# Layer 2's preparation of the states taken into the sixteen steps of its experts, with a new table of search steps

## What is computed

```
x = layer0(x)              # delta-rule attention, three cycles of a coupling net as gate
x = layer1(x)              # two blocks: time mix, windowed attention, gated FFN
# layer 2
u  = silu(conv4(x_proj_half));  sg = silu(other half)
dt, B, C = rmsnorm(x_proj @ u)          # 64 + 16 + 16 rows
dt = softplus(dt_proj @ dt + b);  du = dt * u
h_n = scan(exp(dt * A_n) * h_n + du * B_n),  y = sum_n h_n * C_n     # 16 states n
experts = sum_e w2_e(silu(w1_e x) * (w3_e (gate_e x)))               # 4 experts, 4 chunks each
x = x + silu(experts) * out_proj((y + D u) * sg)
# layer 3: 16 heads; of every score row only the 25 largest stay (found as 4 x "eight largest")
```

## Time and profile before

| what | value |
|---|---|
| median of 3 runs | 5127.44 us (5120.69 to 5140.48) |
| profiled execution, own time | 5138.43 us |
| its span | 5136.6 us |
| mean granted clock of TensorE | 0.837 of 2.4 GHz |
| busy over the span | TensorE 3962.0 us (77%), VectorE 3993.4 (78%), ScalarE 2973.6 (58%), GpSimd 2537.6 (49%) |

### The profile page before, as it was taken

One profiled execution on the slowest core, in us unless ns is written; L12 is line 12 of the kernel. 1 busy time (PEld: TensorE's weight loads), 2 busy tenths in 40 slices (PEclk: granted clock), 3 DMA queues, 4 the chain that ended last, 5 costly groups with the idle time before them and its releaser, 6 DMA issues. The chain is left out here.

```text
span 5136.6 us, 59306 instructions
## 1 busy us (share of the span) xinstructions
PE 3962.0 (77%) x17112; PEld 1870.6 (36%) x17112; DVE 3993.4 (78%) x7866; ACT 2973.6 (58%) x5751; POOL 2537.6 (49%) x2332
## 2 busy tenths in 40 slices
PE   7776878878877777867788687886888778787676
PEld 2332344323443244422444234432344324342233
DVE  4326797877978788786888779887887868978698
ACT  4444666656665566655666566665666556665543
POOL 1204465445645355463654536544555535646365
PEclk9887889888888898978889798988888888997655
DMA  2000000000000000000000000000000000000000
GB/s 82 1 25 3 3 1 25 1 3 3 1 26 0 3 3 1 25 1 5 1 1 25 3 3 1 25 1 3 3 1 25 1 3 3 1 25 1 3 1 3
DMA packets 8147, 44.15 MB, mean 9 GB/s; under 512 B 864, under 2 KB 864, under 8 KB 7392
## 3 DMA queue, kind: packets, MB, share of 16 engines
q1 hardware_dynamic: 7776, 39.89, 2.0%
HBM read 37.52 MB, written 2.36 MB: 8 GB/s over the span
## 5 line engine op out<-in xcount | busy, mean ns | idle before, releaser
L2031 DVE MAX8 m<-top 128x8 f32<-128x512 f32 x2048 | 1295.2, 680 | 6.1 <-ACT top L1965 5.9
L2094 POOL TENSOR_SCALAR top<-top,m 128x512 f32<-128x512 f32 x512 | 819.3, 1600 | 791.8 <-DVE m L2031 682.1
L2035 DVE MATCH_REPLACE8 top<-m,top 128x512 f32<-128x512 f32 x1536 | 1027.1, 677 | 0.4
L2100 POOL TENSOR_TENSOR top<-top 128x512 f32<-128x512 f32 x512 | 655.2, 1280 | 20.1 <-ACT top L1973 1.7
L290 PE MATMUL bank<-arena,weights 128*128 128x512 f32 (+5 forms) x992 | 526.1, 649 | 100.1 <-DVE arena L1217 44.8
L290 PE MATMUL bank<-arena,consts 128*128 128x512 f32 (+1 forms) x864 | 546.2, 722 | 56.1 <-POOL arena L1638 30.5
L1904 PE MATMUL bank<-consts,top 128*128 128x128 f32 x2048 | 394.8, 325 | 230.1 <-POOL top L2100 173.9
L290 PE MATMUL bank<-arena 128*64 128x128 f32 (+3 forms) x3200 | 469.6, 370 | 55.8 <-ACT arena L1080 51.3
L1904 PEld LDWEIGHTS bank<-consts,top 128*128 128x128 f32 x2048 | 279.7, 165 | 499.0 <-POOL top L2100 351.2
L1980 ACT ACTIVATE top<-bank 128x512 f32<-128x512 f32 x512 | 305.5, 597 | 263.0 <-PE bank L1904 262.7
L1965 ACT ACTIVATE top<-bank 128x512 f32<-128x512 f32 x512 | 302.9, 593 | 251.2 <-PE bank L290 172.8
(11 more groups left out here) (300 smaller groups left out, 6484.2 us busy)
## 6 DMA issues: line engine op xcount, KB each, us to landing
arena<-experts_dram SPq DMA_DIRECT2D x32, 768.0 KB, 6.6
weights<-weights_dram SPq DMA_DIRECT2D x1, 6013.0 KB, 22.5
hold<-x_dram SPq DMA_DIRECT2D x9, 256.0 KB, 2.7
out_dram<-x_out SPq DMA_DIRECT2D x9, 256.0 KB, 3.4
consts<-consts_dram SPq DMA_DIRECT2D x1, 1759.5 KB, 8.7
rot<-consts_dram SPq DMA_DIRECT2D x1, 1024.0 KB, 24.3
weights<-weights_dram SPq DMA_DIRECT2D x1, 969.0 KB, 4.8
```

Source lines behind the costliest of these rows:

```text
L2031: nc.vector.max(m8[:, slot(p, e), k], src).then_inc(SB["top"], 1)
L2035: nc.vector.match_replace(wk_[e], m8[:, slot(p, e), k], sc[slot(p, e)] if k == 0 else wk_[e], -3e38).then_inc(SB["rest"], 1)
L2094: nc.gpsimd.tensor_scalar(pp[e], sc[slot(p, e)], m8[:, slot(p, e), TOPK // 8, 0:1], None, ALU.is_ge).then_inc(SB["kept"], 1)
L2100: nc.gpsimd.tensor_tensor(pp[e], pp[e], ex[e], ALU.mult).then_inc(SB["pp"], 1)
```

## The change

It takes the preparation's instructions out of the seven hops and puts each into one of the moe steps, on bank A[3], which the moe steps use for `spread` only. To make room, `spread` and `xg` move from k == 1 to k == 2 of each expert, `h1`, `hg`, `gate` and one `xg` buffer get other memory (dt and du may no longer lie under `h1` and `hg`), and one more copy takes x_proj out of PSUM (L1458 of the changed kernel, `xp_sb`). Own steps are now 185. The table `SEARCH` is new: the 46 search steps that lay in moe and preparation (33 and 13) are 42 in moe; before layer 2's moe steps come 190 search steps instead of 189, and behind them 26 steps start at the 233rd instead of the 236th.

```diff
-SEARCH = ("0210020250210111101110113034221131412302512101102011202012023110m50112251100421133202211010010021201"
+SEARCH = ("0201020250210111100210120080232032311404303100021201221101023a0e352010411100421132320003011101012011"
...
                 L.cn = [L.xp_flat[:, 0:T], L.xp_flat[:, T:2 * T], L.carve()]
+                L.h1, L.hg = L.cn[0:2], [L.carve(), L.carve()]
...
-                    if k == 1 and e + 1 < NE:
+                    if k == 2 and e + 1 < NE:
+                        if e:
+                            pe.wait_ge(*S("xr_ln", 1) if e == 1 else S("dt_relu", 2))
                         spread(e + 1)
...
+                if n == 3:
+                    pe.wait_ge(*S("xg", 2))
+                    for c in range(2):
+                        r = mm(A[3][0:96], W("l2_xproj", lo=96 * c, n=96), L.u2[:, c], c == 0, c == 1)
+                    r.then_inc(S["xproj"], 1)
+                if n == 4:
+                    pe.wait_ge(*S("xsq", 1))
+                    mm(A[3][0:96], C("rms"), L.xr[0:96]).then_inc(S["xms"], 1)
+                if n == 7:
+                    pe.wait_ge(*S("xd", 1))
+                    mm(A[3][0:96], C("three"), L.xd[0:96]).then_inc(S["three"], 1)
+                if n in (8, 9):
+                    pe.wait_ge(*S("left", 1) if n == 8 else S("dt_relu", 1))
+                    mm(A[3], W("l2_dt", lo=128 * (n - 8), n=128), L.xd[0:64]).then_inc(S["dtp"], 1)
                 yield "moe"
```

On ScalarE Copy and Square come at n == 4, Ln and Exp of the norm at n == 5, the first part at n == 8, Abs and Relu at n == 9 and 10, and at n == 11:

```diff
+                if n == 11:
+                    a.wait_ge(*S("mid", 1))
+                    act(bf_parts[32:64], bf_mid[32:64], ACT.Copy).then_inc(S["parts_b"], 1)
+                    table(LN, TANH)
+                    for c in range(2):
+                        a.wait_ge(*S("dt_abs", c + 1))
+                        act(L.cv[:, c], L.cv[:, c], ACT.Exp, scale=-1.0).then_inc(S["dt_exp"], 1)
+                    table(LN)
+                    for c in range(2):
+                        a.wait_ge(*S("dt_exp", c + 1))
+                        act(L.cv[:, c], L.cv[:, c], ACT.Ln, bias=C("one")).then_inc(S["dt_ln"], 1)
```

More of the change, by code:

```diff
@@ L1326, in __init__ @@
                 L.sq, L.rs, L.left = spare[0:3]
-                L.gate = L.carve()
-                L.xg = [spare[4], L.xr]
+                L.gate = L.hg[0]
+                L.xg = [spare[4], L.cn[2]]
                 L.lx = Norm(S2, "xn", x[:], [S1("x_new", 1)], xn[:], L.sq, L.rs)
@@ L1455, in l2_act @@
                     act(L.h1[n % 2], A[1], ACT.Silu).then_inc(S["h1"], 1)
+                if n == 4:
+                    a.wait_ge(*S("xproj", 1))
+                    act(L.left[0:96], A[3][0:96], ACT.Copy).then_inc(S["xp_sb"], 1)
+                    act(L.xr[0:96], A[3][0:96], ACT.Square).then_inc(S["xsq"], 1)
+                if n == 5:
+                    table(LN)
+                    a.wait_ge(*S("xms", 1))
+                    act(L.rs[0:96], A[3][0:96], ACT.Ln, bias=C("eps6", 96)).then_inc(S["xr_ln"], 1)
+                    a.wait_ge(*S("xr_ln", 1))
+                    act(L.rs[0:96], L.rs[0:96], ACT.Exp, scale=-0.5).then_inc(S["xrs"], 1)
+                if n == 8:
+                    a.wait_ge(*S("three", 1))
+                    act(bf_parts[:], A[3][0:96], ACT.Copy).then_inc(S["parts_a"], 1)
+                if n in (9, 10):
+                    c = n - 9
+                    a.wait_ge(*S("dtp", c + 1))
+                    act(L.cv[:, c], A[3], ACT.Abs, bias=W("l2_dt_b", lo=c, n=1)).then_inc(S["dt_abs"], 1)
+                    act(L.dt[:, c], A[3], ACT.Relu, bias=W("l2_dt_b", lo=c, n=1)).then_inc(S["dt_relu"], 1)
+                if n == 9:
+                    a.wait_ge(*S("left", 1))
+                    act(bf_mid[:], L.left[0:96], ACT.Copy).then_inc(S["mid"], 1)
+                if n == 11:
[5 more added lines that the diff above has]
+                        act(L.cv[:, c], L.cv[:, c], ACT.Exp, scale=-1.0).then_inc(S["dt_exp"], 1)
+                    table(LN)
+                    for c in range(2):
+                        a.wait_ge(*S("dt_exp", c + 1))
+                        act(L.cv[:, c], L.cv[:, c], ACT.Ln, bias=C("one")).then_inc(S["dt_ln"], 1)
                 yield "moe"
@@ L1459, in l2_act @@
             act(L.gate, A[0], ACT.Silu).then_inc(S["gate"], 1)
[L1460 to L1491 removed]
+            a.wait_ge(*S("hg", NE * FCH))
             for n in range(NS):
@@ L1573, in l2_dve @@
                     tt(L.hg[n % 2], L.h1[n % 2], A[2], ALU.mult).then_inc(S["hg"], 1)
[L1574 removed]
+                    if n % FCH == 2 and n // FCH + 1 < NE:
                         gate(n // FCH + 1)
[L1576 to L1594 removed]
+                if n == 6:
+                    v.wait_ge(*S("xrs", 1))
+                    v.wait_ge(*S("xp_sb", 1))
+                    stt(L.xd[0:96], L.left[0:96], W("l2_xln"), L.rs[0:96], ALU.mult, ALU.mult).then_inc(S["xd"], 1)
+                if n == 8:
+                    v.wait_ge(*S("xd", 1))
+                    v.wait_ge(*S("parts_a", 1))
+                    tt(L.left[0:96], A[3][0:96], bf_parts[:], ALU.subtract).then_inc(S["left"], 1)
+                if n == 10:
+                    v.wait_ge(*S("mid", 1))
+                    v.wait_ge(*S("left", 1))
+                    tt(bf_parts[64:96], L.left[64:96], bf_mid[64:96], ALU.subtract).then_inc(S["parts_c"], 1)
+                if n == 12:
+                    v.wait_ge(*S("dt_ln", 2))
+                    tt(L.dt, L.dt, L.cv, ALU.add).then_inc(S["dt"], 1)
+                if n == 13:
+                    v.wait_ge(*S("dt", 1))
+                    tt(L.du, L.dt, L.u2, ALU.mult).then_inc(S["du"], 1)
+                yield "moe"
             v.wait_ge(*S("du", 1))
+            v.wait_ge(*S("down", NE * FCH))
             for n in range(NS):
@@ L1629, in l2_pool @@
             nc.gpsimd.memset(L.xp[:, :, T + 1:T + 3], 0.0).then_inc(S["pads"], 1)
-            yield from idle("hop busy busy hop hop hop " + "moe " * (NE * FCH + 1) + "hop hop hop hop hop hop hop")
+            yield from idle("hop busy busy hop hop hop " + "moe " * (NE * FCH + 1))
             def weigh(n):
```

76 lines of the change are left out of this document (4 added, 72 removed).

## The result

The changed kernel took 5185.95 us (median of 4 runs, 5182.03 to 5190.13), the kernel before beside it 5126.3 (4 runs): ratio 1.0103, 95% interval 1.0079 to 1.0127. It is 1.0% slower, where 1.3% faster was forecast. The profiled execution took 5182.03 us with a span of 5180.2.

The account below looks back on a forecast made before the run. No engine fills a 611 us round; VectorE, fullest, is busy 497. Saving 14.2 less 5.6 given back is 8.6 us a round, 60 over seven, plus 8 in the first block: 5059 us, range 5010 to 5120 (8 in 10).

Parts of the forecast that it names:

- 71 / 0.92 = 77.5 us: First gate product to first state's product, each round: VectorE's 71 us of work at 92% busy, against 91.7 before.
- the 14.2 us: Forecast saving a round in the rewritten stretch, first gate product to first state's product: 91.7 - 77.5.
- The 92%: Share of the rewritten stretch its fullest engine was taken to be busy; before, the fullest reached 94%.
- TensorE's 66.6 us: TensorE's counted work in a round's rewritten stretch: moe, search, spread and preparation matmuls, all at 2.4 GHz.
- Clock near 1.00 throughout: Sign expected in the changed profile: TensorE's granted clock near 1.00 over the whole rewritten stretch.
- ScalarE's 65 us: ScalarE's counted work in a round's rewritten stretch, with 17 table loads instead of 11.
- Given back, 5.6 us: Loss a round: 2.4 ahead of the stretch, 2.5 between first state's product and scans, 0.7 for three more tail steps.
- at nothing, between -3 and +3 us: Cost a round of the new table's shuffling of search steps among layers 0 and 1.
- First block, 7.8 us saved: First block: 16.7 us off from last silu to first scan, less 5.2 for TensorE's six matmuls and 3.7 of waits.
- Rival 2: ScalarE's table switches hold the experts' silus: 4.1 us open behind each of eight blocks, 5212 us; chance 0.10.
- drain variant: Each ScalarE table switch adds a wait as long as its load: 8.9 us a round, 5181 us; chance 1 in 100.
- Rival 1: VectorE's list sets the round, so rounds gain nothing and only the first block's 8 us stay: 5119 us; chance 0.18.

Follow-up runs that it names:

- e17: Changed kernel with the old search digits ahead of layer 2's experts, half-sized unneeded matmuls in expert steps 5 to 12, experts' silus as plain copies; ratio 0.9949.
- e14: Changed kernel with the old search digits ahead of layer 2's experts and half-sized unneeded matmuls (128x256) in expert steps 5 to 12; ratio 1.0012.
- e2: Changed kernel with the old search digits ahead of layer 2's experts, no added matmuls; ratio 1.0035 to the kernel before.
- e5: Changed kernel with the experts' 16 silus as plain copies, so no table switch is left among the experts; ratio 1.0041 to the kernel before.
- e6: Kernel before with the experts' 16 silus as plain copies; ratio 1.0006 to the unedited kernel before.
- e8: Changed kernel with the old search digits ahead of layer 2's experts and in the states, new ones only in the expert steps; ratio 1.0024.
- e1: Kernel before with only the search digits ahead of layer 2's experts replaced by the new ones; ratio 1.0056.
- e7: Changed kernel with 3 of the 5 search steps between the first state's product and its scan moved two places on; ratio 1.0135 to the kernel before.
- e16: Kernel before with half-sized unneeded matmuls (128x256) in its expert steps 5 to 12; ratio 1.0020.
- e3: Changed kernel with the preparation's logarithms and exponentials as plain copies and its three table calls dropped; ratio 1.0032 to the kernel before.

## Why the prediction was wrong

**The stretch, "71 / 0.92 = 77.5 us": the step that failed.** It measured 91.7 on average. From the runs, the 14.2 us are: work 2.3 (73.3 on VectorE, not 71; 1.2 of it an item's outputs, which the sum had laid ahead of the stretch and the trace has in it); a chain that leaves VectorE 10.0 us idle even with neither switch nor low clock (e17), where 77.5 - 71 = 6.5 were allowed: 3.5; the switches 88.3 - 83.3 = 5.0 (e14, e17); the low clock, and with it what the digits ahead do to the stretch, 91.7 - 88.3 = 3.4. (Both e14 and e17 hold 3 us of fills, so the last is rather more and the chain's part rather less: e2's best rounds, at 0.98 without fills, took 86.8 us, which would make them 4.9 and 2.0. With the averages of e14 and e17, 89.0 and 83.6, the switches have 5.4.) The switches' part rests on two pairs of runs (e5 with e6, e14 with e17); the chain's part is what is left over, and no run separates its links, such as the one bank that preparation and gates share. The 92% was carried over from a stretch in which TensorE was full at 0.99 and ScalarE was 60% busy; it is no property of an engine's list. As it stands the fullest engine is TensorE, 78.05 of 91.10 = 86%.

**TensorE's 66.6 us "at 2.4 GHz".** The count is low by 6 even near full clock: e2's third round has 72.5 busy at 0.98. Part of that is the way of counting, for a pair of matmuls shows 1.02 us where the next starts after 0.86. In the changed kernel the 1.2 GHz make it 78. "Clock near 1.00 throughout" failed with 0.90 to 0.91: filling all engines made TensorE's stops shorter, and the low clock came all the same, beside dense work.

**ScalarE's 65 us** measured 62.9. Right; that three nearly full engines in one chain would still pack was the error.

**Given back, 5.6 us.** At the states 3.2 were forecast, 3.1 measured: right in size, partly by luck. 2.5 were laid to search steps between product and scans, but by e8 the first state is 2.1 us longer without them, through the wait for the gate's silu and the load. The forecast named that wait but did not charge it, though the kernel before has none there. What the digits add stands in the second state. Ahead, 2.4 for one more search step and the outputs was forecast; the profiles show 3.6, though the outputs did not move.

**The table ahead "at nothing, between -3 and +3 us".** By the ratios the digits ahead cost 0.56 to 0.68%, 4 to 5 us a round, part of it paid in the stretch. With the 2.4 us charged above taken off, some 2 us are left: not nothing, but within the bounds stated. That the cause is the clock at which the experts begin is seen in e1's rows, not shown by an edit.

**First block, 7.8 us saved.** From first gate product to first scan it is 410.8 - 349.1 = 61.7 for 415.4 - 349.9 = 65.5: 3.8. The timeline there, other rows left out:

```profile
397.53 2.07 PE L290 MATMUL bank<-xn,arena 128*128 128x512 f32 x2 [2.64 <-ACT arena L1455]
...
408.12 0.60 ACT L1491 ACTIVATE arena<-bank 128x512 f32<-128x512 f32 x1 [2.22 <-PE bank L290]
...
410.83 2.34 DVE L1609 TENSOR_TENSOR_SCAN arena<-bank,arena 128x512 f32<-128x512 f32 x2 [1.16 <-ACT bank L1500]
```

From the gate's silu to the first scan it is 2.7 us, as forecast; the missing 4.0 lie ahead. TensorE's stops there, 0.58, 0.99 and 2.64 us, make 4.2 for the 3.7 forecast. The low clock was not in the sum: e7, whose first block is the same code, had 0.99 for 0.94 there and reached the first product in 56.9 us instead of 59.3, so it is worth about 2.4. About 1 us is open.

**The rivals.** Rival 2, the switches, comes nearest in time (5212, drain variant 5181), and its place is right; its price was not: 5.0 us a round, where 4.1 for each of eight blocks would be 33. The drain variant fell: the load at 2848.47 is followed by Exp at 2849.76, 1.29 us later, with no further wait. The Trainium skill's figure (ScalarE: Activation LUTs, What ACT_TABLE_LOAD costs) of some 1.38 us more for a switch is seen nowhere here; its 1283 ns for the load is. Rival 1 was right only in that rounds gained nothing: by it VectorE's list sets the round, but VectorE's idle time in the stretch rose.

## What to carry to other kernels

Work is not hidden by being laid among full engines: ask for each moved wait what stands in order behind it on every engine, and count the table loads on both sides of a moved exponential. A stretch in which TensorE is the fullest engine should be costed at both clocks, since seven stops of at most 1.02 us were followed by 1.2 GHz here; the low clock cost some 2 us beside little matmul work (e16) and some 3 to 5 beside dense work. And a table that shuffles the order elsewhere is a change of its own: time it alone (e1) before the gain of the main edit is spent on it.

## What was not expected of the hardware

- Behind 15 us with stops of at most 1.02 us each the granted clock fell to 1.2 GHz, and identical instructions in other rounds of the same execution kept 2.4 GHz for most of the place (e2: 0.98 and 0.93 over the stretch). The stops alone do not say when it falls.
- A kernel with more work was faster: 3 us of unneeded matmuls a round, 1.0103 to 1.0053, though two thirds of that lie where nothing was edited, and in two other pairs of kernels the fills gained nothing clear.
- In the first block, of which nothing up to there was edited, the first gate product comes at 349 to 350 us in some executions and at 355 to 361 in others (changed kernel 349.1, e3 358.3, same code and digits up to there). Why is open, and with one profile of each kernel it can't be said whether it goes with the kernel or with the execution.
- VectorE's du took 1.22 us where GpSimd was idle (every round of the changed kernel) and 2.20 beside it (every round before). The Trainium skill (SBUF — State Buffer, SBUF: two separate sides) has VectorE and GpSimd take turns at a shared port; the two durations agree with that.
